# A selective scan, a noisy feed-forward layer and attention on one core: x kept in f32, and the sums over states taken in pairs of tiles

## The reference, cut to what matters

```python
xn = layernorm(x)                          # (4096, 256)
Bm = xn @ W_B.T + b_B                      # (4096, 16 states)
Cm = xn @ W_C.T + b_C
Delta = softplus(xn @ W_Delta.T + ...)     # (4096, 1)
A_bar = exp(A * Delta)                     # per channel and state
B_bar = 1 / A * (A_bar - 1) * Bm
state = state * A_bar + xn * B_bar         # token after token
y     = sum over the states of state * Cm  # (4096, 256)
x     = x + y
```

## Time and profile before

| | us |
|---|---|
| median of three runs (lowest, highest) | 3477.23 (3475.85, 3478.11) |
| the profiled execution | 3478.46 |
| its span in the trace | 3476.6 |
| PE, DVE busy | 3330.3 (96%), 3260.1 (94%) |
| ACT, POOL busy | 2718.5 (78%), 830.4 (24%) |

### The profile page before, as it was taken

One profiled execution on the slowest core, in us unless ns is written; L12 is line 12 of the kernel. 1 busy time (PEld: TensorE's weight loads), 2 busy tenths in 40 slices (PEclk: granted clock), 3 DMA queues, 4 the chain that ended last, 5 costly groups with the idle time before them and its releaser, 6 DMA issues.

```text
span 3476.6 us, 59741 instructions
## 1 busy us (share of the span) xinstructions
PE 3330.3 (96%) x22826; PEld 1192.6 (34%) x22852; DVE 3260.1 (94%) x4960; ACT 2718.5 (78%) x4991; POOL 830.4 (24%) x707
## 2 busy tenths in 40 slices
PE   6788888989999999999999999999999999999999
PEld 3222222542333333333333333333333333333334
DVE  7899999589999999999999999999999999999943
ACT  6766665756888888888888888888888888888865
POOL 3899998662000000000000000000000000000004
PEclk9999999988999999999999999999999999999999
DMA  2000001052020120202020202112020202020011
GB/s 65 1 10 0 1 1 49 31 149 30 6 33 13 28 30 10 33 6 33 8 33 6 33 6 33 25 16 33 6 33 6 36 6 33 6 33 6 8 55 49
DMA packets 53678, 87.11 MB, mean 25 GB/s; under 512 B 13200, under 2 KB 40464, under 8 KB 49232
## 3 DMA queue, kind: packets, MB, share of 16 engines
q1 hardware_dynamic: 53200, 82.77, 12.6%
q10 hardware_dynamic: 192, 0.52, 0.1%
HBM read 53.37 MB, written 21.23 MB: 21 GB/s over the span
## 4 chain that ended last, share of the span: by engine, by line
PE 81%; DVE 10%; issue 4%; POOL 1%; ACT 1%; DMA 0%; DVEq 0%; SPq 0%; POOLq 0%; ACTq 0%
PE banks L1493 29%; PE banks L1450 16%; PE banks L1445 15%; PE banks L1408 11%; DVE arena L999 5%; PE banks L553 3%; DVE arena L969 3%; PE banks L1406 2%; PE banks L805 1%; DVE arena L1666 1%; DVE arena L980 1%; PE banks L797 1%; PE banks L1515 1%; POOL arena L1122 0%; POOL arena L1113 0%
## 5 line engine op out<-in xcount | busy, mean ns | idle before, releaser
L1649 DVE TENSOR_REDUCE arena<-banks 128x1 f32<-128x512 f32 x4032 | 2503.7, 683 | 19.1 <-PE banks L1408 15.5
L1623 ACT ACTIVATE arena<-banks 128x512 f32<-128x512 f32 x4096 | 2114.9, 602 | 417.0 <-PE banks L1445 409.5
L1445 PE MATMUL banks<-arena 64*128 64x512 bf16 x4032 | 1245.8, 379 | 0.0
L1450 PE MATMUL banks<-arena 35*128 35x512 bf16 x4032 | 1207.2, 378 | 0.6 <-DMA arena<-max_rows 0.4
L1493 PE MATMUL banks<-arena 128*32 128x512 f32 x8192 | 1090.8, 605 | 0.0
L1406 PE MATMUL banks<-arena 64*128 64x512 bf16 x2048 | 789.2, 387 | 22.9 <-DVE arena L1666 20.2
L1408 PE MATMUL banks<-arena 64*128 64x512 bf16 x2048 | 786.9, 386 | 0.6 <-DVE arena L1649 0.6
L1445 PEld LDWEIGHTS banks<-arena 64*128 64x128 bf16 x4032 | 375.8, 93 | 391.7 <-PE banks L1450 5.7
L1408 PEld LDWEIGHTS banks<-arena 64*128 64x128 bf16 x2048 | 188.2, 93 | 796.6 <-DVE arena L1649 792.4
L1450 PEld LDWEIGHTS banks<-arena 35*128 35x128 bf16 x4032 | 358.0, 93 | 157.7 <-ACT arena L1623 8.7
L1373 POOL TENSOR_TENSOR arena<-arena 64x512 f32<-64x512 f32 x64 | 81.2, 1268 | 1191.6 <-DMA arena<-arena 1157.2
(11 more groups left out here) (137 smaller groups left out, 1730.7 us busy)
## 6 DMA issues: line engine op xcount, KB each, us to landing
arena<-qk_parts SPq DMA_DIRECT2D x242, 128.0 KB, 7.1
qk_parts<-arena SPq DMA_DIRECT2D x32, 384.0 KB, 2.6
arena<-arena SPq DMA_DIRECT2D x63, 128.0 KB, 2.3
x_res<-in_x SPq DMA_DIRECT2D x8, 512.0 KB, 7.9
arena<-in_trig SPq DMA_DIRECT2D x2, 2048.0 KB, 9.0
arena<-qk_parts SPq DMA_DIRECT2D x64, 64.0 KB, 10.9
att_t<-arena SPq DMA_DIRECT2D x128, 32.0 KB
arena<-att_t SPq DMA_DIRECT2D x8, 512.0 KB, 5.5
```

Of the source, the lines that this page charges most:

```text
L1445: return nc.tensor.matmul(sc[:, (4 * t + j) % SB, :], k, q, start=(j == 1), stop=(j != 1))
L1450: return nc.tensor.matmul(sc[:, (4 * t + j) % SB, :], k, q, start=(j != 1), stop=(j == 1))
L1623: nc.scalar.activation(prob[:, t % PBUF, j * CH:(j + 1) * CH], sc[:, n % SB, :], ACT.Exp, scale=SCALE).then_inc(exp_done, 1)
L1649: nc.vector.tensor_reduce(part_max[:, b % 2, u // NC, u % NC:u % NC + 1], mx[:, unit_bank(b, u), :], AXX, ALU.max).then_inc(dve_read, 1)
```

## The change

x stays in f32 from stage one on, and the three bf16 parts with all steps that make them go. The spread is one f32 matmul to a bank instead of three bf16 ones. Tiles take the channels in another order (`channels`), in which consecutive tiles fall into different column groups. The sums of two consecutive tiles are issued together, bank by bank, after the second tile's hc. hc has four buffers instead of two.

```diff
-                def what_hi_leaves(i):                      # POOL, 8 chunks
-                    nc.gpsimd.tensor_tensor(rest[:, i % 2], xnt[:, i % 2], mem.xp[:, 0, :, cols(i)],
-                                            ALU.subtract).then_inc(rest_ready, 1)
-                def low(i):                                 # DVE, 8 chunks
-                    nc.vector.tensor_tensor(mem.xp[:, 2, :, cols(i)], rest[:, i % 2], mem.xp[:, 1, :, cols(i)],
-                                            ALU.subtract).then_inc(lo_ready, 1)
                 def copy_turned(i):
                     act.wait_ge(t_ready, i + 1)
-                    if i >= 2:
-                        act.wait_ge(proj_ready, i - 1)
-                        act.wait_ge(rest_ready, i - 1)
-                    nc.scalar.activation(xnt[:, i % 2], tp[:], ACT.Copy).then_inc(xnt_ready, 1)
-                def high(i):  ...
-                def middle(i):  ...
+                    nc.scalar.activation(mem.x_t[:, :, cols(i)], tp[:], ACT.Copy).then_inc(xnt_ready, 1)
...
+def channels(n):
+    return n % NJ // NJH * NJH + n % 4 * 4 + n % NJH // 4
...
-            c, j = n // NJ, n % NJ
+            c, j = n // NJ, channels(n)
...
             for b in range(SC // CH):
-                for part in range(NPART):
-                    last = nc.tensor.matmul(
-                        x_bank(n)[:, b * CH:(b + 1) * CH], mem.spread[:, j % NJH, :],
-                        mem.xp[:, part, j // NJH, c * SC + b * CH:c * SC + (b + 1) * CH],
-                        start=(part == 0), stop=(part == NPART - 1))
+                last = nc.tensor.matmul(
+                    x_bank(n)[:, b * CH:(b + 1) * CH], mem.spread[:, j % NJH, :],
+                    mem.x_t[:, j // NJH, c * SC + b * CH:c * SC + (b + 1) * CH], start=True, stop=True)
...
-            turns = jj == 2 and k > 0
-            if turns:
+            if n % NJH == 2 and k > 0:
                 turn_y(k, n + 5)
             for m in spreads_before_gather(n):
                 spread_x(m)
-            pe.wait_ge(hc_done, n + 1)
+            if n % 2 == 1:
+                sum_pair(n - 1, n)
+
+        def sum_pair(*pair):
+            n, k = pair[1], pair[1] // NJH
+            pe.wait_ge(hc_done, n + 1)
...
             for b in range(SC // CH):
-                last = nc.tensor.matmul(
-                    yb[32 * g:32 * g + 32, b * CH:(b + 1) * CH], mem.gather[:, j, :],
-                    hc[:, n % 2, b * CH:(b + 1) * CH], start=(r == 0), stop=(r == 3),
-                    tile_position=(0, 32 * g))
+                for m in pair:
+                    g, r = channels(m) % NJH // 4, channels(m) % 4
+                    last = nc.tensor.matmul(
+                        yb[32 * g:32 * g + 32, b * CH:(b + 1) * CH], mem.gather[:, channels(m), :],
+                        hc(m)[:, b * CH:(b + 1) * CH], start=(r == 0), stop=(r == 3), tile_position=(0, 32 * g))
...
-            if n >= 2:
-                pool.wait_ge(y_done, n - 1)
-            nc.gpsimd.tensor_tensor(hc[:, n % 2, :], st[:, n % 2, :], mem.c_rep[:, cols(n)],
+            if n >= 4:
+                pool.wait_ge(y_done, n - 3)
+            nc.gpsimd.tensor_tensor(hc(n), st[:, n % 2, :], mem.c_rep[:, cols(n)],
                                     ALU.mult).then_inc(hc_done, 1)
```

More of the change, by code:

```diff
@@ L142, in norm_and_project @@
         xn = place(mem, 112, [2, TPC, D])
-        xnt = place(mem, 120, [2, DH, CH])
-        rest = place(mem, 128, [2, DH, CH])
         std = sb("np_std", [P, NT, 1], F32)
@@ L151, in norm_and_project @@
         (loaded, consts, pool_step, gather_step, sums_done, stats_done, std_ready, rstd_ready, xn_ready, t_ready, xnt_ready,
-         hi_ready, rest_ready, mid_ready, lo_ready, proj_ready, proj_read, neg_ready, exp_ready, ln_ready, bias_ready,
+         proj_ready, proj_read, neg_ready, exp_ready, ln_ready, bias_ready,
          soft_added, angles_loaded, angle_step, table_step) = make_sems(
-            nc, ctx, "np", "loaded consts poolstep gatherstep sums stats std rstd xn t xnt hi rest mid lo proj projread neg "
+            nc, ctx, "np", "loaded consts poolstep gatherstep sums stats std rstd xn t xnt proj projread neg "
             "exp ln bias softadded anglesloaded anglestep tablestep")
@@ L205, in _ @@
                 steps.link(nc.gpsimd.memset(mem.carry[:], 0.0))
-                def what_hi_leaves(i):
-                    pool.wait_ge(hi_ready, i + 1)
-                    if i >= 2:
-                        pool.wait_ge(lo_ready, i - 1)
-                    nc.gpsimd.tensor_tensor(rest[:, i % 2], xnt[:, i % 2], mem.xp[:, 0, :, cols(i)],
-                                            ALU.subtract).then_inc(rest_ready, 1)
-                for i in range(NC):
-                    what_hi_leaves(i)
             @block.vector
@@ L242, in normalise @@
                     last.then_inc(xn_ready, 1)
-                def low(i):
-                    dve.wait_ge(mid_ready, i + 1)
-                    nc.vector.tensor_tensor(mem.xp[:, 2, :, cols(i)], rest[:, i % 2], mem.xp[:, 1, :, cols(i)],
-                                            ALU.subtract).then_inc(lo_ready, 1)
                 def minus_abs(q):
@@ L302, in _ @@
                         stats(i + 4)
-                    if i >= 1:
-                        low(i - 1)
                     if i in (3, 5, 7):
@@ L313, in _ @@
                         softplus(1)
-                low(NC - 1)
                 minus_abs(NSC - 1)
@@ L367, in _ @@
                         copy_turned(i + 1)
-                    high(i)
                     if i >= 1:
-                        middle(i - 1)
                         outputs(i - 1)
@@ L380, in _ @@
                         logs(1)
-                middle(NC - 1)
                 outputs(NC - 1)
@@ L407, in _ @@
                         for h in range(DH):
-                            last = nc.tensor.matmul(pb[:, i % 2, n, :], w_bcd[:, h, n, :], xnt[:, i % 2, h, :],
+                            last = nc.tensor.matmul(pb[:, i % 2, n, :], w_bcd[:, h, n, :], mem.x_t[:, h, cols(i)],
                                                     start=(h == 0), stop=(h == DH - 1))
@@ L619, in scan_to_projection @@
     st = place(mem, 144, [2, SC])
-    hc = place(mem, 152, [2, SC])
+    hc_pairs = (place(mem, 152, [2, SC]), place(mem, 40, [2, SC]))
     ysb = mem.soft[:, 0, :]
@@ L628, in scan_to_projection, with hc @@
     LATE = NSC - 2
+    def hc(n):
+        return hc_pairs[n // 2 % 2][:, n % 2, :]
     def x_bank(n):
@@ L708, in spread_x @@
         def spread_x(n):
-            c, j = n // NJ, n % NJ
+            c, j = n // NJ, channels(n)
             if n > 1:
                 pe.wait_ge(w_done, n if n > 3 else n - 1)
-            if n > NJH and j % NJH == 7:
+            if n > NJH and n % NJH == 7:
                 pe.wait_ge(x_added, n // NJH)
             for b in range(SC // CH):
-                for part in range(NPART):
-                    last = nc.tensor.matmul(
-                        x_bank(n)[:, b * CH:(b + 1) * CH], mem.spread[:, j % NJH, :],
-                        mem.xp[:, part, j // NJH, c * SC + b * CH:c * SC + (b + 1) * CH],
-                        start=(part == 0), stop=(part == NPART - 1))
+                last = nc.tensor.matmul(
+                    x_bank(n)[:, b * CH:(b + 1) * CH], mem.spread[:, j % NJH, :],
+                    mem.x_t[:, j // NJH, c * SC + b * CH:c * SC + (b + 1) * CH], start=True, stop=True)
             last.then_inc(xr_ready, 1)
@@ L733, in scan_tile @@
         def scan_tile(n):
-            j, k, jj = n % NJ, n // NJH, n % NJH
-            turns = jj == 2 and k > 0
-            if turns:
+            k = n // NJH
+            if n % NJH == 2 and k > 0:
                 turn_y(k, n + 5)
@@ L740, in scan_tile @@
                 spread_x(m)
+            if n % 2 == 1:
+                sum_pair(n - 1, n)
+        def sum_pair(*pair):
+            n, k = pair[1], pair[1] // NJH
             pe.wait_ge(hc_done, n + 1)
-            if n == 0:
+            if n == 1:
                 pe.wait_ge(w_done, 4)
-            if jj == 0 and k > 0:
+            if n % NJH == 1 and k > 0:
                 pe.wait_ge(y_copied, k)
-            g, r = jj // 4, jj % 4
             for b in range(SC // CH):
-                last = nc.tensor.matmul(
-                    yb[32 * g:32 * g + 32, b * CH:(b + 1) * CH], mem.gather[:, j, :],
-                    hc[:, n % 2, b * CH:(b + 1) * CH], start=(r == 0), stop=(r == 3),
-                    tile_position=(0, 32 * g))
-            last.then_inc(y_done, 1)
+                for m in pair:
[3 more added lines that the diff above has]
+                        hc(m)[:, b * CH:(b + 1) * CH], start=(r == 0), stop=(r == 3), tile_position=(0, 32 * g))
+                    if b == SC // CH - 1:
+                        last.then_inc(y_done, 1)
         def out_bias():
@@ L852, in decay_less_one @@
                 return
-            m, j = pool_before(n), n % NJ
```

(11 more changed lines are left out.)

## The result

The changed kernel takes 3510.38 us (median of four runs, 3508.99 to 3513.49) beside 3477.11 for the kernel before (median of four runs here): slower by 33 us, ratio 1.0097 (95% interval 1.008 to 1.0115). The forecast was 3474.3, range 3464 to 3496.

The account below looks back on a forecast made before the run. DVE's queue was taken to set the scan body's pace, POOL 3% behind. Terms -8.8 - 1.5 + 1.1 + 7.0 - 0.7 = -2.9 from the median 3477.23 gave 3474.3 us, range 3464 to 3496.

Parts of the forecast that it names:

- Rival 3: Scan body: new gaps of 2.3 us throw PE to 1.2 GHz once a half; +28 us, 3502; chance 0.11.
- Stage one: Before the scan: without roundings and remainders PE keeps its rhythm and DVE's last instruction ends at 68.1, not 76.9; -8.8 us.
- Start of the scan: First tiles: spreads 5 and 6 go ahead of the first pair, against a later first product; -1.5 us.
- The +1.1 for the two longer idle stretches: Spreads after idle time before 136.34 (0.8) and at the second quarter's softplus (0.3) come later; +1.1 us.
- Body: Scan body: the f32 spread fits DVE's rhythm except at three kinds of place; +1.0 in each of seven halves, +7.0 us.
- tile 9: Once a half only `own_u` lies between two `times_b` and a pair between spreads 8 and 9; +0.7 beyond the existing 0.43 wait.
- the pair that POOL holds up: Scan body, product of tile 11 done late by POOL: the spread behind that pair is late by +0.1 us.
- The common `times_b` behind a bare scan: Scan body: the f32 spread is ready at T + 3.18, DVE comes at T + 3.37; fits with 0.2 to spare.
- Rival 4: f32 spread a little too slow, over 2.17 us from release to product; at 2.3, +10 us, 3484; chance 0.14.
- Rival 5: A pair's sums don't run side by side, 3.66 us instead of 1.83; +69 us, 3543; chance 0.08.
- End: After the scan: tile 126's sum moves behind the first feed-forward products, unit 0's turn comes earlier; -0.7 us.

Follow-up runs that it names:

- experiment 1: Changed kernel, but each tile's sum issued by itself behind its own hc instead of in pairs: 3484.6 us.
- experiment 3: Changed kernel plus one added 512-column f32 matmul by a matrix of zeros every two tiles, while PE waits for DVE: 3478.6 us.
- experiment 9: Changed kernel with y turned inside yb and each tile's sum issued by itself (tiles 0 and 1 of a half together), no added matmul: 3474.5 us.
- experiment 2: Kernel before with only the channel order, the paired sums and three hc buffers; stage one and bf16 spread stay: 3491.4 us.
- experiment 10: As experiment 3, but the added matmul has 128 columns instead of 512: 3509.3 us.
- Experiment 5: As experiment 3, plus three more f32 matmuls at the end of stage one, whose result nobody reads: 3476.5 us.

## Why the prediction was wrong

**The step that failed** is the one on the clock: "The longest gap of the new order in the body is 2.3 us", set beside the gap of 2.71 us of the earlier trace rows behind which the clock had stayed at 2.4. By it the sum holds no term for a lower clock in the body. The gaps were right (2.37 and 2.14; the one of 4.54 us at the softplus of the second quarter had a term of its own), but the inference from the earlier trace rows, that a gap under 2.71 us leaves the clock alone, was not: the granted clock was 0.91 from 150 to 550 us, and DVE waited 37.3 us for spreads there instead of 2.6. The trace of before held the counterexample, a sum at half clock behind a gap of 2.37 us (PE, in order of time):

```profile
593.28 3.53 PE L749 MATMUL banks<-arena 128*32 128x512 f32 x4 [2.37 <-POOL arena L1122]
```

The third rival's "or less where PE has been idle more often" was all that I made of it. Experiments 1, 3 and 9, in which PE has more to do while it would wait for DVE, keep the clock at 1.00. The page of the Trainium skill (TensorE: Matmul & The Clock Gate, Part 1) has the clock follow how busy the array has lately been. In direction these three runs and experiment 2 agree with it, and it was the better guide than the longest gap. The amount of work over a long stretch doesn't order the clocks, though: 258.84 us of 400 in experiment 2 with 0.94, 301.85 in the changed kernel with 0.91, 315.25 in experiment 10 with 0.92. At which spread the clock falls no run explains.

**Rival 3** named what happened, half clock in the body, at 0.11. Its trigger, the gaps of 2.3 us once a half, was not right: the clock also fell behind gaps of 2.14 and, in experiment 10, 1.80 us. Its price was near and a little low, +28 for one fall in a half: the trace shows 26 slow spreads in eight halves, about three in a half, and 38.5 us of waits at or behind them, and the difference that added work makes (3510.4 to 3478.6) is 31.8 us. Three slow spreads a half instead of one fall, at about 1.5 us each instead of 3.5: that the totals lie so near is in part luck.

**Stage one**, -8.8: DVE's last instruction ended at 67.7 instead of 76.9, -9.2, and the scan's first spread came 9.6 sooner. Right, and so is the way to it: PE's turn of chunk 7 came at 53.19, where I had 53.61, and the last projections followed without a break.

**Start of the scan**, -1.5: the scan of tile 2 starts 9.5 us sooner, 0.3 more than the 9.2 of stage one, where I had 1.5. The spread of tile 5 no longer stands behind the first sum, as said, but DVE still waits 2.08 us for it, since its buffer comes free only with the `times_b` just before, and spread 4 ran at half clock (1.39). I had left out the first of these. Experiment 5 gives the second back. The +1.1 for the two longer idle stretches was about twice too much: in experiment 3 DVE waits 0.33 and 0.50 us at tiles 15 and 16, where the kernel before waits 0.58 once, and 0.23 at tile 36.

**Body**, +7.0: this was for full clock, and experiment 3 comes nearest to it: 1.33 at tile 9 where I had 0.43 + 0.7 = 1.13, twice 0.20 where I had 0.1, and no wait of the pair that POOL holds up. That is 1.3 a half on the kernel before instead of 1.0, so 9.1 instead of 7.0; 0.08 of each place is the spread itself, which I had taken at 1.90, and it took the 1.98 of my high end. From the scan of tile 2 to the last one it takes 506.4 us there against 495.2, +11.1 with all other places, beside my 7.0 + 1.1. The common `times_b` behind a bare scan doesn't wait, as said. Rivals 4 and 5 did not come about: a spread took 1.98 and fitted, a pair took 1.91.

**End**, -0.7: from the last scan's start to the turn of y it was 14.5 instead of 14.9 us, -0.4.

So by its own terms the forecast describes about experiment 3 (3478.6, +0.5 on the kernel before, where I had -2.9). What it lacked was that the work removed from PE had been keeping PE's clock up.

## What to carry to other kernels

Work taken from PE where another engine sets the pace isn't free of risk: if PE then idles more, it may be granted half the clock, and the instruction on which the pacing engine waits takes up to twice as long (the spread here up to 3.78 us instead of 1.98). Read the granted clock of every stage before and price each PE step on the path at both levels. If work can be taken away only where nobody waits for it, leave it, or keep the clock with work whose result isn't used. And a step that only just fits into a rhythm (1.98 us into 2.17) has no cover at the lower clock.

## What the runs showed of the hardware that I had not expected

The clock was not set by the gap right ahead alone: 2.14 us of idle time stood ahead of spreads of 1.98, 2.91 and 3.46 us within one kernel. A matmul by a matrix of zeros keeps the clock as real ones do (3478.6 instead of 3510.4, with 512 columns); one of 128 columns in the same place didn't (3509.3). And two f32 matmuls in different column groups, each over two banks, ran side by side in 1.91 us, against 1.90 for one.
